# A vision-transformer layer on one core: gapless transposes of q and k, bf16 transposes of quantised rows, and a new order

## What is computed

```python
h = concat([cls_tok, cls_token, patches @ W_lin.T + b_lin])           # 64 x 198 x 192
q, k, v = split(layernorm(h) @ w_qkv.T)
attn = softmax(rope(q * scale) @ rope(k).T)                           # 12 heads of 16
h = h + (attn @ v) @ w_proj.T + b_proj
def bitlinear(x, w, g):                    # w: ternary; x: 8-bit steps of each row's maximum
    xn = rmsnorm(x, g)
    return activation_quant(xn) @ weight_quant(w).T
up, gate = split(bitlinear(layernorm(h), w_in, g_in))                 # 192 -> 1024
h = h + bitlinear(silu(gate) * up, w_out, g_out)                      # 512 -> 192
```

## Time and profile before

| what | value |
|---|---|
| median of three runs | 1297.24 us (1286.29 to 1311.62) |
| the profiled execution | 1307.32 us, span 1305.5 us |
| mean granted PE clock in it | 0.966 |
| busy: PE, PEld | 1242.4, 909.2 us |
| busy: VectorE, ScalarE, GpSimd | 959.8, 874.8, 888.1 us |
| DMA engines, mean busy | 28.8% for the main queue |

### The profile page before, as it was taken

How to read it: one execution, slowest core, us unless ns; L and a number is a source line. 1 busy time by engine, 2 the same in 40 slices (tenths; PEclk the granted TensorE clock), 3 DMA queues, 4 the chain that set the end, 5 groups by cost and what they waited for, 6 DMA issues and landing times.

```text
span 1305.5 us, 36845 instructions
## 1 busy us (share of the span) xinstructions
PE 1242.4 (95%) x12526; PEld 909.2 (70%) x12526; DVE 959.8 (74%) x2332; ACT 874.8 (67%) x1553; POOL 888.1 (68%) x1608
## 2 busy tenths in 40 slices
PE   6798999999999999999999999999999999998877
PEld 5566677767777767777767777766777776776556
DVE  1454677878888778888778888777888787886665
ACT  1244677767777767777767777766777777775564
POOL 4544787767777767777776777776777777774243
PEclk8888999999999989999999999998999999997799
DMA  6513232332333323323333323322333332211010
GB/s 176 149 47 84 84 84 74 99 84 72 99 93 106 88 68 104 97 80 96 89 104 84 92 80 94 98 69 73 91 84 92 103 93 71 78 47 49 19 44 25
DMA packets 156522, 109.72 MB, mean 84 GB/s; under 512 B 42281, under 2 KB 155636, under 8 KB 156244
## 3 DMA queue, kind: packets, MB, share of 16 engines
q1 hardware_dynamic: 153764, 104.23, 28.8%
q10 hardware_dynamic: 2576, 3.14, 0.9%
HBM read 66.57 MB, written 10.70 MB: 59 GB/s over the span
## 4 chain that ended last, share of the span: by engine, by line
PE 82%; SPq 7%; DMA 5%; ACT 3%; DVE 2%; issue 1%; POOL 0%; DVEq 0%; ACTq 0%; POOLq 0%
PE turn L507 13%; PE score L569 12%; PE turn L591 11%; PE turn L525 8%; PE turn L618 6%; PE score L548 5%; PE turn L535 5%; PE turn L578 4%; PE turn L626 3%; PE turn L636 3%; PE turn L489 2%; PE turn L599 2%; PE turn L607 2%; PE turn L517 2%; PE turn L600 2%; DMA orec<-rden_kept 2%
## 5 line engine op out<-in xcount | busy, mean ns | idle before, releaser
L895 DVE TENSOR_REDUCE nmax<-score 99x8 f32<-99x1584 f32 x192 | 347.3, 1809 | 98.7 <-PE score L548 93.4
L722 ACT ACTIVATE prob<-score 99x1584 f32<-99x1584 f32 x192 | 286.4, 1492 | 130.4 <-PE score L569 130.1
L507 PE MATMUL turn<-wlin,xp 128*128 128x192 f32 x1188 | 221.8, 339 | 8.2 <-DMA xp<-in_x 8.2
L507 PEld LDWEIGHTS turn<-wlin,xp 128*128 128x128 f32 x1188 | 201.5, 199 | 12.4 <-issue 10.7
L569 PE MATMUL score<-qkT 17*99 17x198 f32 x3072 | 181.7, 351 | 21.2 <-DMA qkT<-nmaxT 11.9
L569 PEld LDWEIGHTS score<-qkT 17*99 17x99 f32 x3072 | 117.7, 163 | 85.4 <-issue 69.3
L591 PE MATMUL turn<-prob,vaug 99*32 99x198 f32 x3072 | 156.5, 346 | 0.0
L525 PE MATMUL turn<-wqkv,xT 96*128 96x384 f32 x396 | 148.7, 499 | 2.3 <-ACT xT L691 2.3
L1081 POOL TENSOR_TENSOR yg<-early,gout 128x512 f32<-128x512 f32 x99 | 125.5, 1268 | 24.1 <-ACT yr L774 16.6
L591 PEld LDWEIGHTS turn<-prob,vaug 99*32 99x32 f32 x3072 | 92.1, 113 | 41.9 <-issue 17.7
L618 PE MATMUL turn<-winq,xiT 96*128 96x512 bf16 x396 | 102.0, 380 | 5.5 <-ACT xiT L745 5.5
(11 more groups left out here) (92 smaller groups left out, 2518.2 us busy)
## 6 DMA issues: line engine op xcount, KB each, us to landing
xp<-in_x SPq DMA_DIRECT2D x63, 588.0 KB, 5.5
tab<-joined SPq DMA_DIRECT2D x98, 112.0 KB, 3.2
orec<-rden_kept SPq DMA_DIRECT2D x192, 49.5 KB
out<-h SPq DMA_DIRECT2D x99, 96.0 KB, 1.8
onum<-osb SPq DMA_DIRECT2D x64, 99.0 KB, 2.6
vaug<-vt SPq DMA_DIRECT2D x30, 148.5 KB
onum<-osb SPq DMA_DIRECT2D x64, 49.5 KB, 3.2
qkT<-nmaxT SPq DMA_DIRECT2D x192, 3.1 KB
```

Of the source, the lines that this page charges most:

```text
L507: last = pe.matmul(turn[:, k, 0:D], xp[:, c, place:place + TILE], wlin[:, c, :], start=(c == 0), stop=(c == KC - 1))
L722: act.activation(prob[:, :, 4 * g:4 * g + 4, :].rearrange("p t r n -> p r t n"), score[0:TT, :, 0:2 * TOKENS].rearrange("p r (t n) -> p r ...
L895: dve.tensor_reduce(nmax[:, b % 2, :, 4 * g:4 * g + 4].rearrange("p t r -> p r t"), score[0:TT, :, 0:2 * TOKENS].rearrange("p r (t n) -> p ...
```

## The change

Four things are changed together.

1. `qkp` holds the 384 columns of q and k without filler. Three transposes (in place of six) put eight heads on 128 partitions, 16 each. ScalarE copies the 384 columns to a new buffer `qkd`, and SP spreads it by DMA (`place_qk`) to the even partitions of `qkT`, two transfers a tile, four where the ring wraps. The odd partitions are set once, zeros for q and ones for k; the maxima now go to partition 31 of each quadrant. The contraction is 31 rows in `max_scores` and 32 in `exp_scores`.
2. ScalarE takes the rounding constant off in a second pass (`even_x`, `even_y`) that writes bf16 rows `xi` and `yi`; these are transposed as bf16 with a bf16 identity, and the copies out of PSUM are plain.
3. The order of the work is rewritten on all engines, and the tables of half steps with it. The ring of h has 24 tiles in place of 20, and `fy` 8 columns in place of 4.
4. The loops begin at step -1. The number of the last step stays.

```diff
-            top.append(max(top[-1] + 1 if top else 0, 2 * (final_tile(b) + 3) + 2))
-        turn.append(top[-1] + 1)
+            top.append(max(top[-1] + 1 if top else 0, 2 * (final_tile(b) + 4) + 2))
+        turn.append(top[-1])
...
-            soft.append(max(soft[-1] + 1 if soft else 0, turn[-1] + 1))
-        out.append(soft[-1] + 8)
+            soft.append(max(soft[-1] + 1 if soft else 0, turn[-1] + 2))
+        out.append(soft[-1] + 7)
...
+            def place_qk(i):
+                if i == 0:
+                    sp.wait_ge(qkT_cleared, 2)
+                sp.wait_ge(qkT_copied, i + 1)
+                over = (TILE * (i + 1) - 1 - QRING) // TOKENS
+                if over >= 0:
+                    sp.wait_ge(st_ready, 3 * over + 3)
+                for place, lo, n in pieces(TILE * i, TILE, QRING):
+                    for half in range(2):
+                        sp.dma_start(qkT[0:128:2, half:2 * GROUPS:2, place:place + n],
+                                     qkd[64 * half:64 * half + 64, i % 2, :, lo:lo + n]).then_inc(qk_placed[i % 2], 16)
...
-                k = take(("qkT", i), 2, qkT_copied, Q_COPIES[i])
-                for side in range(2):
-                    for g in range(GROUPS):
-                        head = side * HEADS + 4 * g
-                        last = pe.transpose(turn[:, k + side, g * TILE:(g + 1) * TILE],
-                                            qkp[:, i % 2, head:head + 4, :].rearrange("p h d -> p (h d)"),
-                                            ident[:, :])
+                k = take(("qkT", i), 1, qkT_copied, i + 1)
+                for c in range(GROUPS):
+                    last = pe.transpose(turn[:, k, c * TILE:(c + 1) * TILE], qkp[:, i % 2, c * 128:(c + 1) * 128],
+                                        ident[:, :])
...
-                        rows = slice(32 * r, 32 * r + DH)
+                        rows = slice(32 * r, 32 * r + 31)
...
-                        rows = slice(32 * r, 32 * r + DH + 1)
+                        rows = slice(32 * r, 32 * r + 32)
...
-                    last = pe.transpose(turn[:, k, c * TILE:(c + 1) * TILE], yr[:, i % 2, c * 128:(c + 1) * 128],
-                                        ident[:, :])
+                    last = pe.transpose(turnb[:, k, c * TILE:(c + 1) * TILE], yi[:, i % 2, c * 128:(c + 1) * 128],
+                                        identb[:, :])
...
+            def even_y(i):
+                act.wait_ge(yr_ready, i + 1)
+                if i >= 2:
+                    act.wait_ge(yiT_ready, i - 1)
+                act.activation(yi[:, i % 2, :], yr[:, :], ACT.Copy, bias=-MAGIC).then_inc(yi_ready, 1)
...
+            dve.memset(qkT[:, 0:GROUPS, :], 0.0).then_inc(qkT_cleared, 1)
+            dve.memset(qkT[:, GROUPS:2 * GROUPS, :], 1.0).then_inc(qkT_cleared, 1)
...
             def round_qkT(i):
-                pool.wait_ge(qkT_copied, Q_COPIES[i])
+                pool.wait_ge(qk_placed[i % 2], qk_count(i))
```

More of the change, by code:

```diff
@@ L47 @@
 TBUF = 4
+FBUF = 8
 FIRST_TABS = 4
-HRING = 20
+HRING = 24
 VSLOT = 3
@@ L115, in token_runs, with qk_count @@
     return runs
+def qk_count(i):
+    return sum(32 * len(pieces(TILE * n, TILE, QRING)) for n in range(i % 2, i + 1, 2))
 def beyond(i):
@@ L271, in build @@
         rope_done = sem("rope_done")
+        qkT_cleared = sem("qkT_cleared")
         qkT_ready = sem("qkT_ready")
         qkT_copied = sem("qkT_copied")
+        qk_placed = [sem(f"qk_placed{p}") for p in range(2)]
         qkT_rounded = sem("qkT_rounded")
@@ L427, in _ @@
             load(XSLOT)
-            for s in range(STEPS):
-                for b in at(OUT_AT, 2 * s):
-                    keep_rden(b)
-                for i in tile_at(s - 6):
-                    place_v(i)
-                for b in at(OUT_AT, 2 * s):
-                    place_rec(b)
[L435 to L445, removed]
-                    place_max(b)
-                for b in at(NMAX_AT, 2 * s - 3):
-                    place_max(b)
-                for i in at(PROJ_AT, s - 9):
-                    store(i)
+            for s in range(-1, STEPS):
+                for b in at(OUT_AT, 2 * s + 5):
+                    place_o(b)
+                for b in at(NMAX_AT, 2 * s - 1):
+                    place_max(b)
+                for b in at(OUT_AT, 2 * s + 4):
+                    place_o(b)
+                for i in tile_at(s - 4):
+                    place_qk(i)
+                for b in at(OUT_AT, 2 * s + 3):
+                    place_rec(b)
+                for i in tile_at(s - 4):
+                    place_v(i)
+                for b in at(NMAX_AT, 2 * s):
+                    place_max(b)
+                for b in at(OUT_AT, 2 * s + 5):
+                    keep_rden(b)
+                for b in at(OUT_AT, 2 * s + 4):
+                    keep_rden(b)
+                for i in tile_at(s + 1):
+                    prepare(i)
+                for i in at(PROJ_AT, s - 7):
+                    store(i)
+                for b in at(OUT_AT, 2 * s + 4):
+                    place_rec(b)
             for p in range(TBUF):
@@ L667, in _ @@
                 for n in at(EXP_AT, 2 * s):
-                    weigh_values(n)
+                    exp_scores(n)
+                for i in at(PROJ_AT, s):
+                    project_out(i)
+                for i in tile_at(s - 3):
+                    project_v(i)
+                for i in tile_at(s - 2):
+                    transpose_xn(i)
+                for b in at(NMAX_AT, 2 * s):
+                    transpose_max(b)
                 for n in at(MAX_AT, 2 * s + 1):
                     max_scores(n)
+                for i in tile_at(s):
+                    embed(i)
+                for i in at(PROJ_AT, s - 7):
+                    ffn_out(i)
                 if s >= TILES + LATE:
```

237 lines of the change are left out of this document (119 added, 118 removed).

## The result

| | before | after |
|---|---|---|
| median of the runs beside each other | 1293.1 us (4 runs, 1286.3 to 1311.6) | **1249.7 us** (4 runs, 1244.1 to 1252.1) |
| ratio, 95% interval | | **0.963 (0.958 to 0.968)** |
| profiled execution: its time, span | 1307.3, 1305.5 us | 1250.5, 1248.7 us |
| mean granted clock of TensorE | 0.966 | 0.979 |

A forecast was written before the change was run, and what follows sets the result against it. PE was taken as the bound, filling an 11.87 us step. Terms -36.6 -32.7 +19 +7 = -43 us took the profiled 1307.3 to 1264; 10 less for the median gave 1254 us, range 1225 to 1285.

The forecast's parts named there:

- Points 1 and 2: PE: three q/k transposes fewer, 0.37 us a tile (-36.6 us); bf16 transposes of quantised rows, 0.33 a tile (-32.7 us).
- Rival D: PE: bf16 transposes are slow, 0.28 us each without overlap, giving 1378 us; chance 0.02.
- Point 3: ScalarE: two more passes and a smaller copy, net +0.82 us a tile, 9.7 us a step, covered by PE's 11.17.
- Point 4: SP: two more q/k transfers a tile, issues 6.7 to 8.0 us a step; landing hidden if place_qk comes in the first half.
- The thinnest place of the schedule: SP: place_qk's spot in the step, where a landing 3 us after issue is hidden only in the first half.
- Point 5: Remade order on PE: +0.2 us a step over 94 steps, +19 us, about half from score banks; ends 0 and 66.
- Point 6: Fill and drain: attention starts a step later, last ffn_out seven steps behind its projection; +7 us, from 0 to 12.
- the 18 us of disturbances: Middle of the run: four disturbances where PE waits for a DMA or work behind one, 955.4 us against 937.7.
- A: Rival: everything fits, the order meets each gap and the four disturbances go; about 1216 us, chance 0.15.
- B: Rival: ScalarE and VectorE hand over late, PE waits 0.5 to 0.8 us a step; about 1296 us, chance 0.14.
- C: Rival: q and k land late, PE waits for GpSimd's rounding and the clock falls; 1344 us, chance 0.10.

The follow-up runs named there:

- e11: The kernel after with the ScalarE pass that writes yi made twice, 0.62 us more a tile: 1255.8 us, ratio 0.972 to the kernel before.
- e1: The kernel after with f32 quantised rows as before, without the second ScalarE passes: 1269.8 us, ratio 0.980 to the kernel before.
- e5: The kernel after with f32 rows and its three q/k transposes done twice, so new order with PE's old work: 1286.8 us, ratio 0.993 to before.
- e8: The kernel after with place_qk moved down SP's list, behind reciprocals' spread, v, maxima and reciprocals' store: 1406.3 us, ratio 1.081 to before.
- e4: The kernel before with only the gapless q and k and their DMA, GpSimd's rounding and the attention's table one step later: 1424.5 us, ratio 1.100.
- e7: The kernel after with the feed-forward matmuls (ffn_in) behind both weighings instead of between them: 1257.0 us, ratio 0.969 to the kernel before.
- e3: The kernel before with only the bf16 rows and their second ScalarE passes, in the old order: 1307.4 us, ratio 1.004.
- e10: Old order with bf16 rows alone, plus four filler matmuls between the exponents' scores of the last steps: 1278.6 us, ratio 0.990 to before.
- e6: The kernel after with the loads of x issued from ScalarE's queue in place of SP's: 1268.3 us, ratio 0.977 to the kernel before.
- e9: The kernel after with place_rec, for images of an even half step, behind the next step's place_qk on SP: 1267.5 us, ratio 0.981 to before.

## Why the prediction was right, point by point

**Points 1 and 2 (transposes).** Forecast 0.37 and 0.33 us a tile, measured 0.33 and 0.31 in the mean quiet step; a f32 transpose is 0.14 us when three stand alone, not 0.123 as in a run of six, and a bf16 one 0.055 to 0.08 where I took 0.07. The bf16 price was the estimate from the nearest row and held. Rows of the contraction cost nothing, as taken. Rival D, slow bf16 transposes, is ruled out by these rows. The Trainium skill (TensorE: Matmul & The Clock Gate, Back-to-back issue gap) has about 81 ns for a bf16 matmul of 128 columns: four of `yi` take 0.08 each and agree, two of `xi` take 0.055 and do not.

**Point 3 (ScalarE).** Covered, as forecast, and e11 shows that more would be too. The size was wrong: I had 955 us busy, and it is 871.2, less than before. The two passes that write bf16 are shorter than the f32 ones I took them from (618 and 352 ns against 711 and 443), and the busy time counts overlap once: the groups `yi` and `xi` add 96.1 us, while e1, which lacks them, is busy 805.2 us, only 66 less. And the new order packs ScalarE's instructions closer: from before to e5, which has no added pass, its busy time falls from 874.8 to 815.3 us, and only 33 of that is the smaller copy of q and k. So the mean duration of a pass can overstate what one more adds. It need not: in e11 the repeated pass waits for the first, and 99 of 0.62 us add 61.

**Point 4 (SP).** "The thinnest place of the schedule" was right: e8 turns it into +157 us. In e4 the new transfers cost 10% by another way, through the maxima that they hold up. In the kernel after itself the GpSimd wait is there and small:

```profile
POOL qkTr L1108 <- DMA qkT<-qkd: 25.8, 10, 5.0
```

**Point 5 (the order), +0.2 us a step.** The size was right, the reason wrong. Quiet steps came to 11.36 us against 11.17 + 0.2 = 11.37, and e5 against before gives 0.15 for the order alone. But it is not waiting for score banks: in 124.73 us of quiet steps PE is busy 124.50, and in the whole run it waits 7.7 us for ScalarE's prob where I had 10 to 30.

```profile
520.02:644.75 124.73, 124.50 (x1331) 88.30 (x1328) 104.13 (x255) 95.72 (x193) 97.76 (x178) 1.00 0.44 112
```

It lies in the pieces into which the list is now cut. Median times from start to start, e5 against before: the weighing +0.14 us a step, the q/k projection +0.09, the projection +0.08, the transposes of xn +0.07, v -0.06. They sum to more than 0.15; a part of the old order's quiet step is waiting. Why a group's time depends on its neighbours is not shown. e7 brought the weighing's part back and lost it at the neighbours.

**Point 6 (fill and drain), +7 us, is where the sum failed**: the ends are 29.1 us shorter. The drain of before ran at a mean clock of 0.91 with only 127 us of busy PE in 151; I read its rows in a step with the clock at 1.00 and never asked for the clock of the whole stretch. The new order fills it better (e5: 141.9 at 0.96), and the fill ran at 0.95 in place of 0.91. e3 and e10 show how much hangs on that: their drains differ by 24.4 us, and their programs by some filler.

**What I left out made up for it.** I kept the 18 us of disturbances as they were. They grew to 30.0. My reading: a transfer late by a fixed time is hidden by long steps and not by short ones, and then the clock falls. The same place in e5 and in after shows it once; that it holds for the other disturbances is argued. SP issues the three transfers of maxima in 3.25 us in both; e5 first (start, us, queue, operation):

```profile
309.13 3.25 SPq L435 DMA_DIRECT2D qkT<-nmaxT x3
```

```profile
306.37 3.25 SPq L437 DMA_DIRECT2D qkT<-nmaxT x3
```

In both PE's scores start 9.8 us behind the first of these issues, so the maxima are equally late. But PE has come to them 8.4 us behind it in e5 and 6.1 in after: the 2.3 us between are what three or four steps save at 0.64 us each. In e5 its wait here is the longest for maxima in the whole run, and from 310 to 320 it keeps the clock:

```profile
318.89 0.93 PE L593 MATMUL score<-qkT 32*99 32x198 f32 x16 [1.38 <-DMA qkT<-nmaxT]
```

In after the wait is 3.68 us, the next scores take 1.66 us in place of 0.93, and the embedding behind them 3.80 in place of 2.22:

```profile
316.15 1.66 PE L595 MATMUL score<-qkT 32*99 32x198 f32 x16 [3.68 <-DMA qkT<-nmaxT]
...
321.61 3.80 PE L537 MATMUL turn<-wlin,xp 128*128 128x192 f32 x12
```

Windows of PE, e5 and then after:

```profile
310.00:320.00 10.00, 8.62 (x101) 1.00 0.26 61
```

```profile
310.00:320.00 10.00, 6.32 (x59) 0.73 0.30 72
```

The sum then reads: quiet -38.8 (forecast 79 x -0.5 = -39.5), disturbances +11.1 (0), ends -29.1 (-4: the +7, and the 20 tiles whose transposes lie there), together -56.8 in the profiled runs against a forecast of -43. So for the profiled execution I had 1264 us, and it took 1250.5: two misses, of 11 and 25 us, cancelled in part and left 14. The median came within 5 us because I then took off 10, the distance of the profiled execution of before from its median; in after that distance was 0.8. The quiet steps were forecast with reason. That 1254 was so near was in good part luck. What makes SP's issues slow at those few places stays open: neither taking x off the queue (e6) nor moving the reciprocals (e9) shortened them.

**Rivals.** A (1216) had no disturbances and no cost of the order, and has both wrong. B (1296) had PE waiting 0.5 us or more in each step; there is no such wait. C did not come: in the kernel after PE waits 4.7 us for the rounded q and k, and only e8, which moves `place_qk`, brings it about.

## What to carry to other kernels

Cost the quiet step by start-to-start times (here they added up to a tenth of a microsecond over 79 steps), and price the rest apart: the stretches where PE is not full by their own granted clock, and the late transfers, whose slack is the step itself, so that of 50 us saved in the steps 24 came back. A saving and the order that carries it belong together: one half alone in the old order gained nothing, the other, with its transfers at one place of SP's old list, lost 10%.

## What the runs showed of the hardware that I had not expected

- Less work on PE can make the end slower. With shorter bf16 transposes and gaps of 1.37 us, the granted clock of the last 173 us was 0.74; four more matmuls of filler in a step brought it to 0.92 and 148.9 us (one profiled run each; 1.4% between the kernels' ratios).
- Gaps of the same length do not have the same effect: with two gaps of 1.70 us behind exponents' scores, 12 to 15 us apart, the granted clock was 0.61 and 0.64 over 20 us in the profiled runs of e9 and e11, and in that of the kernel after, behind the first of the two, it fell for some four microseconds. Their programs differ a little, so whether this is chance is open.
- An f32 transpose costs 0.123 us in six and 0.14 in three, and a weighing 1.48 us in one piece and 1.62 in two; the change of group has a price that neither the mean of one nor the waits show.
- Two transfers a tile, moved down SP's list from ahead of four other kinds of transfer to behind them, made the kernel 157 us slower.
